# Delta-rule attention: values convolved on VectorE, the head of the next chunk's inverse in the present step, and the queues reordered

## The reference

```python
mixed = jnp.einsum('bth,ch->btc', hidden_states, qkv_w)          # q, k, v of all heads
...
x = lax.conv_general_dilated(x, conv_w, window_strides=(1,), padding=[(KCONV - 1, 0)], feature_group_count=CONV_DIM, dimension_numbers=('NCH', 'OIH', 'NCH'))
...
beta = jax.nn.sigmoid(bb)
g = -jnp.exp(A_log) * jax.nn.softplus(aa + dt_bias)
alpha = jnp.exp(g)
...
def step(S, inp):
    S = S * alpha_t[..., None, None]
    kv = jnp.einsum('bhk,bhkv->bhv', k_t, S)
    S = S + jnp.einsum('bhk,bhv->bhkv', k_t, (v_t - kv) * beta_t[..., None])
    o_t = jnp.einsum('bhk,bhkv->bhv', q_t, S)
...
var = jnp.mean(jnp.square(o), axis=-1, keepdims=True)
o = o * lax.rsqrt(var + EPS) * norm_w
o = o * (z * jax.nn.sigmoid(z))
out = jnp.einsum('btv,hv->bth', o.reshape(b_, t_, VAL_DIM), out_w)
```

## Time and profile before

| | us |
|---|---|
| three runs | 8073.55, 8070.39, 8049.4 (median 8070.39) |
| the profiled execution | 8045.66 |
| its span, first to last instruction | 8043.8 |
| busy PE, PEld | 6799.7 (85%), 4816.6 (60%) |
| busy DVE, ACT, POOL | 5751.5 (72%), 3577.8 (44%), 2800.7 (35%) |
| mean granted PE clock | 0.892 of full speed |

### The profile page before, as it was taken

One profiled execution on the slowest core, in us unless ns is written; L12 is line 12 of the kernel. 1 busy time (PEld: TensorE's weight loads), 2 busy tenths in 40 slices (PEclk: granted clock), 3 DMA queues, 4 the chain that ended last, 5 costly groups with the idle time before them and its releaser, 6 DMA issues. The chain is left out here.

```text
span 8043.8 us, 271416 instructions
## 1 busy us (share of the span) xinstructions
PE 6799.7 (85%) x118712; PEld 4816.6 (60%) x118712; DVE 5751.5 (72%) x10171; ACT 3577.8 (44%) x6436; POOL 2800.7 (35%) x1921
## 2 busy tenths in 40 slices
PE   7999789999998898898998998998997798445566
PEld 3444478888886566666665665665664555345434
DVE  6666379999997786786885885885886577842366
ACT  3555245555554565564664664664664222210121
POOL 0110023332332673673773773773772000011000
PEclk8999599999999999999999999999998899555557
DMA  0000000000000321221221221221220000000000
GB/s 15 1 1 1 2 6 5 4 4 4 4 3 10 78 73 48 69 75 44 73 74 43 73 75 42 76 75 42 76 76 17 16 1 2 2 3 4 5 0 14
DMA packets 187953, 249.14 MB, mean 31 GB/s; under 512 B 58998, under 2 KB 85493, under 8 KB 185845
## 3 DMA queue, kind: packets, MB, share of 16 engines
q1 hardware_dynamic: 186740, 231.40, 11.0%
HBM read 27.84 MB, written 2.10 MB: 4 GB/s over the span
## 5 line engine op out<-in xcount | busy, mean ns | idle before, releaser
L1702 POOL TENSOR_TENSOR XNT<-XNT 128x1024 f32<-128x1024 f32 x384 | 907.0, 2362 | 317.9 <-DVE XNT L1871 312.8
L1773 PE MATMUL wa_front<-w_wqkv,wa_xT 128*128 128x512 f32 x1920 | 941.4, 614 | 30.0 <-ACT wa_qT L1766 11.1
L1705 POOL TENSOR_TENSOR XNT<-XNT,wa_rnorm 128x1024 f32<-128x1024 f32 x320 | 608.7, 1902 | 256.6 <-ACT wa_rnorm L1728 232.2
L1773 PEld LDWEIGHTS wa_front<-w_wqkv,wa_xT 128*128 128x128 f32 x1920 | 334.7, 194 | 296.6 <-issue 256.7
L1868 DVE TENSOR_TENSOR XNT<-wa_front,w_scaled 128x1024 f32<-128x1024 f32 x320 | 390.3, 1220 | 159.4 <-PE wa_front L1773 159.4
L447 PE MATMUL a0h_ring<-a0h_QT,a0h_KT 32*128 32x512 f32 (+3 forms) x1536 | 443.8, 549 | 14.4 <-ACT a0h_E L565 10.4
L565 ACT ACTIVATE a0h_E<-a0h_ring 128x512 f32<-128x512 f32 (+1 forms) x640 | 320.5, 555 | 279.9 <-PE a0h_ring L447 278.6
L1871 DVE TENSOR_TENSOR XNT<-wa_front,w_scaled 128x512 f32<-128x512 f32 x640 | 409.2, 681 | 0.0
L1878 DVE TENSOR_REDUCE wa_least<-wa_sq 128x16 f32<-128x1024 f32 x320 | 380.0, 1187 | 14.6 <-ACT wa_sq L1720 12.6
L1720 ACT ACTIVATE wa_sq<-wa_front 128x1024 f32<-128x1024 f32 x320 | 326.0, 1020 | 133.4 <-PE wa_front L1773 105.2
L1779 PEld LDWEIGHTS wa_front<-consts,XNT 128*128 128x128 f32 x2560 | 277.9, 142 | 158.4 <-POOL XNT L1705 109.5
(11 more groups left out here) (621 smaller groups left out, 17523.9 us busy)
## 6 DMA issues: line engine op xcount, KB each, us to landing
wa_v_look<-wa_v_all SPq DMA_DIRECT2D x960, 128.0 KB, 2.4
wa_v_look<-wa_v_all SPq DMA_DIRECT2D x640, 64.0 KB, 2.1
wal_v_look<-wal_v_all SPq DMA_DIRECT2D x192, 128.0 KB, 2.4
wal_v_look<-wal_v_all SPq DMA_DIRECT2D x128, 64.0 KB, 2.1
w_wqkv<-in_L_ffn_Wqkv_dram SPq DMA_DIRECT2D x6, 1024.0 KB, 6.4
w_wo<-in_L_ffn_Wo_dram SPq DMA_DIRECT2D x6, 512.0 KB, 6.9
w_wqkv<-in_L_ffn_Wqkv_dram SPq DMA_DIRECT2D x12, 256.0 KB, 7.7
f2w_raw<-in_L_ffn_w_dram SPq DMA_DIRECT2D x48, 64.0 KB, 1.9
```

The lines of the kernel that those rows point to most:

```text
L1702: g.tensor_tensor(rot[:, at], rot[:, at], part[:, at], ALU.add).then_inc(s[summed], 1)
L1705: g.tensor_tensor(rot[:, at], rot[:, at], spread(rnorm[:, at, :], HDW), ALU.mult).then_inc(s[done], 1)
L1773: last = pe.matmul(front[:, first + i, :], x_of(which), wqkv[:, (2 * n + i) * 512:(2 * n + i + 1) * 512], start=True, stop=True)
```

## The change

Eight things change in this stage, and nothing outside it.

- Values are made like keys: one raw product of 512 columns on PE, an eviction by ACT into `hist`, a four-tap convolution on DVE into `vconv`, and a step later four PE transposes and ACT's copy to `vtok`. The shifted copies `xs`, the copies of the weight scaled by taps, and the 16 matmuls go. SP's load of a head's weights also waits for the values convolved two heads before (`vconv_ready`).
- The gram product, N, Nc, lev, and the first XTc and T of chunk j now run late in step j; before, they opened step j + 1. N has two buffers. lev is one product of five levels.
- `ga` is the first thing on DVE; dt is one matmul of 512 columns with the mask `after` as weights; E follows `evict_z(2)`, so E, Estrict and Eincl run in the step's middle, both masks in a row.
- The tangent of the gate stands before `evict_z(6)` as before, but now behind Nc.
- The value convolution is nearly the last of DVE's step, behind y.
- `place` is one masked product on POOL.
- The squares of o and the root (Sqrt) are the last of ACT's step. y is no longer multiplied by rstd; the addition into X does it, as four instructions.
- AT is made early in the step that follows.

Orders after the change, every wait aside:

- PE: kS, `zt(1)`, qk, `tx(1)`, yT, dt, `zt(2)`, qS, `tx(2)`, turned k, raw K, `zt(3)`, u, `tx(3)`, out, `zt(4)`, raw Q, `tx(4)`, o, raw V, `zt(5)`, s, `tx(5)`, gram of j, z, `zt(6)`, turned values, `tx(6)`.
- ACT: `evict_z(1)`, yT, `evict_z(2)`, E, ktok, raw K, `evict_z(3)`, `evict_z(4)`, raw Q, T64, raw V, `evict_z(5)`, T64, Nc, tangent, `evict_z(6)`, vtok, squares, root.
- POOL: newS, sb, Estrict, Eincl, XT's diagonal, lev, hist's tail.
- DVE: ga, kS, R, `grow(1)`, AT, o (qS), `grow(2)`, `convolve(0, 0, 1)`, u, `grow(3)`, uend, `convolve(0, 1, T0)`, `grow(4)`, X, o, `convolve(1, 0, 1)`, round 5, S, N, `convolve(1, 1, T0)`, gate, x6 (round 6), XTc and T, y, `convolve(VC, 0, T0)`, reciprocal.

The diff, cut to the new and changed operations in the order of PE, ACT, POOL, DVE:

```diff
-                def vtok_part(b):
...
-                    for n in range(TAPS):
-                        last = pe.matmul(bank[3][:, b, :], xs[:, q % 2, b, n:n + P], weights(q)[:, V_W + n, :], start=(n == 0),
-                                         stop=(n == TAPS - 1))
-                    if b == G - 1:
-                        last.then_inc(s["vtok_ps"], 1)
...
+                def raw_values():
+                    if j is None:
+                        return
+                    pe.wait_ge(s["raw_copied"], 3 * j + 1)
+                    pe.matmul(flat(bank[0][:]), weights(j)[:, V_W, :], x_of(j), start=True, stop=True).then_inc(s["raw_ps"], 1)
...
+                def turn_values():
...
+                    pe.wait_ge(s["vconv_ready"], q + 1)
+                    if j is not None:
+                        pe.wait_ge(s["raw_copied"], 3 * j + 2)
+                    turn_four(bank[3], vconv[:, q % 2], s["vtok_ps"])
...
+                    pe.matmul(flat(bank[2][:]), c.after, flat(ga[:]), start=True, stop=True).then_inc(s["dt_ps"], 1)
+                zt(2)
...
+                    kj = conv[:, j % 3, K]
+                    pe.wait_ge(s["conv_ready"], 2 * j + 1)
+                    pe.wait_ge(s["raw_copied"], 3 * (j + 1))
+                    four_of(bank[0], lambda b: kj[:, b, :], lambda b: kj[:, b, :], s["gram_ps"])
...
+                    a.activation(E[:], bank[2][:], ACT.Exp).then_inc(s["E_ready"], 1)
...
+                if j is not None:
+                    a.wait_ge(s["N_ready"], j + 1)
...
+                        last = a.activation(Nc[quarter(n)], N[quarter(n), j % 2, :, quarter(n)], ACT.Copy)
+                    last.then_inc(s["Nc_ready"], 1)
+                if q is not None:
                     a.wait_ge(s["z_ps"], q + 1)
                     a.activation(gatez[:, q % 2], bank[5][:], ACT.Tanh, scale=0.5).then_inc(s["tanh_ready"], 1)
                 evict_z(6)
...
+                    g.wait_ge(s["X_ready"], LD * (q + 1))
+                    g.tensor_tensor(XT[:, q % 2].rearrange("p b (k x) -> p b k x", x=32),
+                                    XTc[:].unsqueeze(2).broadcast_to([P, G, 4, 32]),
+                                    c.head_blocks.rearrange("p (k x) -> p k x", x=32).unsqueeze(1).broadcast_to([P, G, 4, 32]),
+                                    ALU.mult).then_inc(s["x4_ready"], 1)
...
+                    if q is not None:
+                        g.wait_ge(s["zt_ps"], LZ * q + 4)
+                        g.wait_ge(s["X_ready"], LD * q + 1)
+                    g.tensor_tensor(lev[:], Nc[:].unsqueeze(1).broadcast_to([P, SMALL, G, 32]),
+                                    small[:, 0:SMALL, :].unsqueeze(2).broadcast_to([P, SMALL, G, 32]),
+                                    ALU.mult).then_inc(s["lev_ready"], 1)
                     if j < CHUNKS - 1:
                         g.wait_ge(s["conv_ready"], 2 * j + 2)
+                        g.wait_ge(s["vconv_ready"], j + 1)
                         if j % BLOCKS < BLOCKS - 1:
...
+                    mine = X[:].rearrange("p (b t) d -> p b t d", b=G)[:, :, e % BLOCKS, :]
+                    for b in range(G):
+                        last = v.scalar_tensor_tensor(out=mine[:, b], in0=bank[2][:, b, :], scalar=rstd[:, b:b + 1],
+                                                      in1=mine[:, b], op0=ALU.mult, op1=ALU.add)
+                    last.then_inc(s["added"], 1)
...
+                if j is not None:
+                    v.wait_ge(s["gram_ps"], j + 1)
+                    v.wait_ge(s["strict_ready"], j + 1)
+                    if j >= 2:
+                        v.wait_ge(s["zt_ps"], LZ * (j - 1))
+                    v.tensor_tensor(N[:, j % 2], bank[0][:], Estrict[:], ALU.mult).then_inc(s["N_ready"], 1)
+                convolve(1, 1, T0)
...
                     v.tensor_copy(XT[0:64, slot, :, 64:P], bank[4][0:64, :, 0:64]).then_inc(s["x6_ready"], 1)
+                if j is not None:
+                    v.wait_ge(s["lev_ready"], j + 1)
+                    if q is not None:
+                        v.wait_ge(s["x4_ready"], q + 1)
+                    v.tensor_tensor(XTc[:], lev[:, 0], ident, ALU.add).then_inc(s["X_ready"], 1)
+                    v.wait_ge(s["X_ready"], LD * j + 1)
+                    if q is not None:
+                        v.wait_ge(s["T64a_ready"], q + 1)
+                        v.wait_ge(s["zt_ps"], LZ * q + 5)
+                    v.transpose(flat(T[:]), flat(XTc[:])).then_inc(s["T_ready"], 1)
+                if r is not None:
+                    v.wait_ge(s["o_done"], r + 1)
+                    v.tensor_tensor(y[:], o[:], gatez[:, r % 2], ALU.mult).then_inc(s["y_ready"], 1)
+                convolve(VC, 0, T0)
                 if r is not None:
...
+                    v.reciprocal(rstd[:], std[:]).then_inc(s["rstd_ready"], 1)
```

More of the change, by code:

```diff
@@ L1212, in keep_weights @@
                     a.wait_ge(s["loaded"], 8 * 16 * (n + 1))
[L1213 to L1218, removed]
                 a.wait_ge(s["w_ps"], 2 * n + 1 + part)
@@ L1225, in keep_weights @@
                 else:
-                    a.activation(into[:, V_W:V_W + TAPS, :], bank[2][:], ACT.Copy).then_inc(s["w_ready"], 1)
+                    a.activation(into[:, V_W, :], bank[2][:, 0, :], ACT.Copy).then_inc(s["w_ready"], 1)
             keep_weights(0, 0)
@@ L1250, in keep_raw @@
                     a.activation(hist[:, n, :, T0:], bank[at][:], ACT.Copy).then_inc(s["raw_copied"], 1)
[L1252 to L1258, removed]
+                evict_z(1)
                 if e is not None:
@@ L1302, in _ @@
                 evict_z(6)
+                if q is not None:
+                    a.wait_ge(s["vtok_ps"], q + 1)
+                    a.activation(vtok[:, q % 2], bank[3][:], ACT.Copy).then_inc(s["vtok_ready"], 1)
+                if r is not None:
+                    a.wait_ge(s["o_done"], r + 1)
+                    for b in range(G):
+                        last = a.activation(osq[:, b, :], o[:, b, :], ACT.Square, accum_out=msq[:, b:b + 1])
+                    last.then_inc(s["msq_ready"], 1)
+                if r is not None:
+                    a.wait_ge(s["msq_ready"], r + 1)
+                    a.activation(std[:], msq[:], ACT.Sqrt, scale=1.0 / P, bias=eps[:]).then_inc(s["std_ready"], 1)
                 keep_weights(next_head(step, 5), 0)
@@ L1363, in _, with convolve @@
                     decay = [spread(of_chunk(decays[:, n], r), P) for n in range(2)]
-                def convolve(n, first, end):
+                def convolve(n, first, end, begin=True):
                     if j is None:
                         return
-                    into = conv[:, j % 3, n]
-                    t = taps[:, j // BLOCKS % 2, 1 - n]
-                    if first == 0:
-                        v.wait_ge(s["raw_copied"], 2 * j + n + 1)
+                    into = vconv[:, j % 2] if n == VC else conv[:, j % 3, n]
+                    t = taps[:, j // BLOCKS % 2, 2 if n == VC else 1 - n]
+                    if first == 0 and begin:
+                        v.wait_ge(s["raw_copied"], 3 * j + n + 1)
                         chain(v.tensor_scalar(into, hist[:, n, :, T0:], t[:, T0:TAPS], None, ALU.mult))
@@ L1388, in grow @@
                     v.transpose(flat(T[:]), flat(XTc[:])).then_inc(s["T_ready"], 1)
-                def place():
-                    for k in range(4):
-                        last = v.tensor_copy(XT[quarter(k), slot, :, quarter(k)], XTc[quarter(k)])
-                    last.then_inc(s["x4_ready"], 1)
-                if q is not None:
-                    v.wait_ge(s["gram_ps"], q + 1)
-                    v.wait_ge(s["strict_ready"], q + 1)
-                    v.tensor_tensor(N[:], bank[0][:], Estrict[:], ALU.mult).then_inc(s["N_ready"], 1)
+                if j is not None:
+                    if j >= 1:
+                        v.wait_ge(s["dt_ps"], j)
+                    v.tensor_tensor(ga[:], c.upto.unsqueeze(1).broadcast_to(four),
+                                    spread(of_chunk(g_all[:], j), P),
+                                    ALU.mult).then_inc(s["ga_ready"], 1)
                 if r is not None:
@@ L1436, in _ @@
                     v.tensor_tensor(o[:], bank[5][:], o[:], ALU.add).then_inc(s["o_done"], 1)
+                convolve(1, 0, 1)
+                if q is not None:
+                    v.wait_ge(s["x_ps"], LX * q + 5)
+                    for lo, hi in BLOCK_PAIRS:
+                        last = v.tensor_copy(XT[quarter(lo), slot, :, quarter(hi)], bank[4][quarter(lo), :, 0:32])
+                    last.then_inc(s["x5_ready"], 1)
+                if r is not None:
                     if r % BLOCKS < BLOCKS - 1:
```

251 lines of the change are left out of this document (98 added, 153 removed).

## The result

The changed kernel takes 8190.3 us (median of 4 runs, 8179.54 to 8192.23) against 8071.65 before (4 runs, 8049.4 to 8073.55): ratio 1.0151, 95% interval 1.0136 to 1.0166. The profiled execution took 8191.32 us, its span is 8189.3. So it is slower, as forecast, and inside the likeliest case's 8120 to 8195, near its upper end.

A forecast was written before the change was run, and what follows sets the result against it. PE was nearly full with DVE close behind, but the new in-order queues would decide: four legs summed to 25.7, taken as 25.6 us against 23.93, 63 x 1.65 = 104 us more, forecast 8160, range 8035 to 8270.

The forecast's parts named there:

- likeliest case: The forecast itself: the four legs make the step 25.6 us, total 8160, own range 8120 to 8195, chance 0.47.
- Legs: Four stretches of one step's path, from one gram product to the next: 6.1, 6.2, 7.6 and 5.8 us.
- the value convolution at the end of DVE's queue: In leg 2, four convolution instructions ahead of the next step's grow(1) put 2.7 us on the path.
- leg 2: From zt(1) to zt(2): DVE's queue ahead of grow(1) sets 6.2 us; PE has 3.4 of work and waits 2.8.
- the masks' hold: In leg 3, POOL's masks hold the K convolution's first DVE instruction; 7.3 to 7.7 us, without the lock 6.7.
- leg 3: From zt(2) to zt(4): 7.6 us, through raw K, the K convolution held by POOL's masks, u and grow(3).
- leg 4: From zt(4) to gram: 5.8 us of PE work without a wait; placing, X additions and third raw copy hidden.
- Marks: Signs listed beforehand: step 25.6, which waits and releasers appear, K's tensor-scalar 1.2 to 1.5 us, DVE and PE near 20.
- Rival 4: The clock falls at PE's wait in leg 2: 2.4 us more per affected step, 8210 to 8310; chance 0.15.
- leg 1: From gram to zt(1): 6.1 us through N, Nc, tangent, Zt6, tx(6), x6, XTc and its transpose; PE waits 1.2.
- Rivals 1 to 3: PE bound, 7860 (faster 0.12); masks don't hold the convolution, 8105 (0.15); chain sum 1.5 too long, 8050 to 8090 (0.11).
- rival 1: PE is the bound and the waits don't arise: 21.0 us a step, -185, total 7860; faster had chance 0.12.

The follow-up runs named there:

- one tap: The changed kernel with the value convolution cut to its first instruction, three of four taps left out; ratio 1.0052 to the kernel before.
- Eincl late: The changed kernel with Eincl's product moved behind `place` on POOL; ratio 1.0104 to the kernel before.
- the last version: The changed kernel with the four moves and one unread 512-column product in PE's wait before tx(6); 8033.73 us, ratio 0.9929 to the kernel before.
- the three moves: The changed kernel with value convolution behind next step's AT, reciprocal just before the additions into X, Eincl behind `place`; ratio 0.9981 to the kernel before.
- the four moves: The three moves plus ACT's root moved behind the next step's `evict_z(1)`; ratio 0.9976 to the kernel before.

## Why the prediction was right

- **Legs.** Forecast 6.1, 6.2, 7.6, 5.8; measured 6.28, 6.08, 7.69, 5.75. Two of the terms were shown by taking them away: the value convolution at the end of DVE's queue (one tap: leg 2 alone shrank) and the masks' hold (Eincl late: leg 3 alone, by 1.05 against the 0.9 between 7.6 and 6.7). The hold is Eincl's by itself, which the prediction's times also give: Estrict over at 4.1 after zt(2), as the convolution could start. The terms listed for leg 3 add to 7.8, a tenth over its stated upper end; 7.69 was measured. Legs 1 and 4 were read in the timeline and not tested by a move.
- **Prices that no row had.** `place` on POOL 1.26 (1.27 said), lev 1.54 (1.6), the four additions into X 1.09 (1.1), R held to 0.99 from 0.68 (0.2 to 0.4 said). `place`, the four additions and the third raw copy, which the prediction put at nothing in leg 4, stayed hidden: it is 5.75.
- **Size.** The step came out 25.71 in the mean for 25.6. That is 112 us in the profiled pair for the 104 forecast. The total of 8160 was 30 too low: 8 by the steps, 16 because it was counted from 8056 and the median before is 8071.65, the rest outside the steps. So the mechanism carried the forecast, but that 8190.3 still lies under 8195 owes something to luck: the two profiled executions differ by 145 us, 33 of them outside the steps, with no cause traced. Likewise the last version's steps would give 63 x 1.27 = 80 us, and the ratio 0.9929 is 57.
- **Marks.** dt was released by ga, zt(2) and zt(4) by the transpose, tx(6) by Zt6, qS' product on DVE waited 1.06 in its step, as listed. PE's longest wait is not zt(2) (1.05) but zt(4) (1.37) and tx(6) (1.22). PE's and DVE's work was 21 us and not 20. DVE's is the held tensor-scalar. PE's is that products which stood one behind another before now stand ahead of a small one or of a wait: qS took 0.89 from its start to the next one's and takes 1.09.
- **Rival 4 was half right.** The clock did fall, to 0.96 over the stage, under the 0.97 that I had named as a sign against me; a low stretch lies in 32 of 63 steps. It did not cost what I worked out: 26 of these begin 3.5 to 5.2 us after N, behind tx(6)'s wait in leg 1 and not in leg 2, where I looked for it; leg 2, where DVE sets the pace, makes good what leg 1 loses, and the step is 25.81 like one at 1.00 (the first two of the three step windows above). The 5 that begin at zt(2) take up to 26.29 (the third), 0.5 more each: 2 to 3 us in all. My price of 2.4 was too high: where the path behind the wait is PE's own, a step with a low stretch pays 1.5 (Eincl late, at zt(2)) or 1.0 (the three moves, at tx(6)).
- **Rivals 1 to 3** fell: PE 84% busy, the tensor-scalar at 1.53, the plain step at 25.80.
- **What the prediction did not see:** with the value convolution out of the way, DVE's next instruction waits 1.3 us for the root at the end of ACT's queue, so moving the convolution alone could return only part. And rival 1's 21 us a step stayed out of reach: with the four moves and the fill it came to 22.62, legs 1 and 4 as long as before.

## What to carry to other kernels

Walk one step around by engine queues before trusting sums of work: here PE and DVE each lost work and the step grew by 1.8 us. Before moving one link off the path, ask what the next instruction in that queue would then wait for (here the root, 1.3 us), and move both. When a chain becomes short enough that TensorE sets the pace again, look at the granted clock of each step: here a product whose result nobody reads, put into the wait behind which the clock fell, was worth 0.77 us a step. Two such products at another wait, in the version whose path ran through DVE, were worth nothing.

## What the runs showed of the hardware

- A low clock is not a cost by itself: the step is 25.81 with a low stretch and 25.80 without where DVE sets the pace, 23.7 against 22.7 where PE does. Nearly all stretches at 0.50 (1.2 of 2.4 GHz) begin 0.4 to 0.7 us behind the start of zt(2), for which PE waited 1.05, or 0.2 to 2.2 behind that of tx(6), after a wait of 1.2 to 1.3, in steps in which PE works over 80% of the time. With tx(6)'s wait filled down to 0.44 all but the first step's are gone, though zt(3) still waits 0.88. The length of one wait does not decide it alone: past the first step of the change no stretch begins behind zt(4), where PE waits longest (1.37). What does decide, these runs don't show. The Trainium skill's "TensorE: Matmul & The Clock Gate", Part 1, says that activity releases the throttle; the filled wait agrees, 1.00 against 0.95 over the same 300 us.
- Engines do not meet at semaphores only. A mask of POOL (Eincl, 1.27) that began 0.02 earlier held a tensor-scalar of DVE to 1.53 with no semaphore between the two; with that mask moved away the same instruction took 0.49, and the one that then met the mask 0.99 for 0.48. The Trainium skill's "SBUF — State Buffer", Who interferes with whom, names tensor_scalar among the instructions that can take the ports which the two engines share, and has whoever issues first take them for the whole instruction, the other waiting; the end 0.28 behind Eincl agrees.
